# Half swaps of a rotating attention: keys ahead of the key spread, queries behind it

## The reference

```python
def _rope(x, base=ROPE_BASE):
    half = D // 2
    inv_freq = 1.0 / base ** (jnp.arange(half, dtype=jnp.float32) / half)
    ang = jnp.arange(S, dtype=jnp.float32)[:, None] * inv_freq[None, :]
    cos, sin = (jnp.cos(ang), jnp.sin(ang))
    x1, x2 = (x[..., :half], x[..., half:])
    return jnp.concatenate([x1 * cos - x2 * sin, x1 * sin + x2 * cos], axis=-1)
...
q = hidden_state @ Wq.T + bq
k = hidden_state @ Wk.T + bk
v = hidden_state @ Wv.T + bv
q = _rope(q)
k = _rope(k)
out = _banded_attention(split(q), split(k), split(v), WINDOW)
return out @ Wo.T + bo
```

## Time and profile before

| | us |
|---|---|
| median of 3 runs | 3945.59 (3945.36 to 3948.0) |
| profiled execution | 3952.28 |
| its span, first to last instruction | 3950.5 |
| first scores of L2a (T = 0) | at 2381.61 |
| scores of T = 30 | at 2633.14 |
| mean granted TensorE clock over the span | 0.929 of full speed |

### The profile page before, as it was taken

The page is one execution under the profiler, slowest core; times in us unless marked ns, Lnnn a source line. Parts: engine busy times, 40 slices in busy tenths (PEclk is TensorE's granted clock), DMA queues, the critical chain, the costliest instruction groups (busy, mean ns, idle before and its releaser), DMA issues. The chain is left out here.

```text
span 3950.5 us, 127503 instructions
## 1 busy us (share of the span) xinstructions
PE 3432.6 (87%) x46648; PEld 2618.2 (66%) x46648; DVE 2964.8 (75%) x6186; ACT 2252.1 (57%) x3856; POOL 1900.4 (48%) x3002
## 2 busy tenths in 40 slices
PE   8996886798899998999986938999989688789985
PEld 6885675465777775888875626888854344457764
DVE  6996995255898886888873476888867588659975
ACT  5775771344444444778862446778844466457653
POOL 6887984655441110224544425762223355357754
PEclk9997995899999998999986968999989799989988
DMA  2012213697000000110004821121112000000001
GB/s 83 29 31 79 66 58 93 187 266 205 20 17 3 1 0 23 52 52 21 17 21 137 255 80 46 48 55 53 52 46 61 15 0 0 0 28 26 26 8 43
DMA packets 321126, 227.48 MB, mean 58 GB/s; under 512 B 53712, under 2 KB 299472, under 8 KB 320720
## 3 DMA queue, kind: packets, MB, share of 16 engines
q1 hardware_dynamic: 261040, 174.96, 15.5%
q0 software_dynamic: 12288, 25.19, 2.1%
q10 hardware_dynamic: 47520, 23.60, 2.0%
HBM read 131.27 MB, written 54.53 MB: 47 GB/s over the span
## 5 line engine op out<-in xcount | busy, mean ns | idle before, releaser
L807 DVE TENSOR_REDUCE L2a_mx<-L2a_psS 128x32 f32<-128x2048 f32 x64 | 146.6, 2291 | 78.1 <-PE L2a_psS L593 78.1
L2501 POOL TENSOR_TENSOR L1a_rs<-L1a_ag,eps 128x1 f32<-128x1 f32 x64 | 13.0, 203 | 397.7 <-DVE L1a_ag L2666 397.7
L807 DVE TENSOR_REDUCE L1x_mx<-L1x_psS 128x32 f32<-128x2048 f32 x64 | 146.6, 2291 | 69.4 <-PE L1x_psS L593 69.4
L1138 POOL DMA_INDIRECT L0f_sorted_x<-X,L0f_IDX x128 | 123.0, 961 | 93.5 <-issue 34.1
L1557 DVE TENSOR_TENSOR L0f_G<-L0f_SG,L0f_psH 128x512 f32<-128x512 f32 x106 | 73.0, 689 | 112.6 <-ACT L0f_SG L1301 70.5
L493 POOL TENSOR_TENSOR L1x_rs<-L1x_mv,eps 128x2 f32<-128x2 f32 x64 | 12.5, 195 | 293.9 <-DVE L1x_mv L862 293.9
L782 ACT ACTIVATE L1x_PR<-L1x_PR 128x2048 f32<-128x2048 f32 x64 | 122.4, 1912 | 53.1 <-DVE L1x_PR L810 53.1
L810 DVE TENSOR_TENSOR L2a_PR<-L2a_psS,L2a_mx 128x2048 f32<-128x2048 f32 x64 | 146.7, 2292 | 7.3
L810 DVE TENSOR_TENSOR L1x_PR<-L1x_psS,L1x_mx 128x2048 f32<-128x2048 f32 x64 | 146.7, 2292 | 7.3
L782 ACT ACTIVATE L2a_PR<-L2a_PR 128x2048 f32<-128x2048 f32 x64 | 122.3, 1912 | 47.1 <-DVE L2a_PR L810 47.1
L719 ACT ACTIVATE L1x_PT<-L1x_psP 128x512 f32<-128x512 f32 x256 | 145.9, 595 | 2.8 <-PE L1x_psP L641 1.1
(11 more groups left out here) (620 smaller groups left out, 11506.1 us busy)
## 6 DMA issues: line engine op xcount, KB each, us to landing
L0f_WB<-in_w12a SPq DMA_DIRECT2D x53, 312.0 KB, 3.8
L0f_XB<-L0f_sorted_x SPq DMA_DIRECT2D x53, 256.0 KB, 4.0
L0f_sorted_y<-L0f_YB ACTq DMA_DIRECT2D x53, 256.0 KB, 3.9
L1m_WB<-in_w12b SPq DMA_DIRECT2D x37, 321.0 KB, 4.0
L1m_XB<-L1m_sorted_x SPq DMA_DIRECT2D x37, 256.0 KB, 4.1
L1m_sorted_y<-L1m_YB ACTq DMA_DIRECT2D x37, 256.0 KB, 4.2
L0x_VS<-in_ctx SPq DMA_DIRECT2D x64, 128.0 KB, 2.8
KB<-L1x_QK SPq DMA_DIRECT2D x256, 32.0 KB, 1.8
```

The source lines that it names most:

```text
L807: nc.vector.tensor_reduce(mx[:, T.u, :], sc, AX, ALU.max).then_inc(S["maxed"].sem, 1)
L1138: nc.gpsimd.indirect_dma_start(out=sorted_x[p][:, :], out_offset=bass.IndirectOffsetOnAxis(ap=IDX[:, k, t:t + 1], axis=0), in_=X[:, t, :], ...
L2501: nc.gpsimd.tensor_tensor(rs[:, A.par, 0:1], ag[:, A.par, 1:2], eps[:, 0:1], ALU.add).then_inc(S["var_eps"].sem, 1)
```

## The change

SyncE's swap becomes a small function that swaps one part, keys (0) or queries (1). In slot T the keys of pair T+2 are swapped first, after a wait for `o_k` of that pair, then comes the spread of pair T+1, then the queries of pair T+2 are swapped, after `o_q`. There are four swap transfers a slot where there were two, each of half the size (64 partitions by 256 values). The key swap counts on a semaphore that this attention did not use (`side_in`), the query swap on the old one (`stored`), and GpSimd's first rotation product waits for the former. The `pace` step (an increment of a semaphore) between SyncE's two waits for the swap is dropped. Other attentions are built without `halves` and keep their order.

```diff
@@ -346,6 +346,12 @@
 
 
             def sync(sp):
+                def swap_halves(M, part, copied, arrival):
+                    made(sp, copied, M.p + 1)
+                    for n in range(2):
+                        here, there = slice(64 * n, 64 * n + 64), slice(64 - 64 * n, 128 - 64 * n)
+                        sp.dma_start(RK[here, M.u, part, 256:512], RK[there, M.u, part, 0:256]).then_inc(parity_sem(arrival, M), 16)
+
                 def slot(T):
                     more = T.c + 4
                     if arrive and T.i is None and 0 <= more < MORE:
@@ -376,6 +382,8 @@
                         made(sp, "f_v", K.p - 1)
                         pace(sp, S)
                         sp.dma_start(CV[:, K.u, :], io["ctxT"][:, bass.ds(K.p * 256, 256)]).then_inc(parity_sem("side_in", K), 16)
+                    if halves and K.ok:
+                        swap_halves(K, 0, "o_k", "side_in")
                     B = T + ahead if turned else K
                     if B.ok:
 
@@ -385,13 +393,7 @@
                         for b in range(HQ):
                             sp.dma_start(KB[b:P:HQ, B.u, b, :, :].rearrange("p s k -> p (s k)"), KT[b:P:HQ, B.u, :]).then_inc(parity_sem("keys_in", B), 16)
                     if halves and K.ok:
-
-                        made(sp, "o_k", K.p + 1)
-                        pace(sp, S)
-                        made(sp, "o_q", K.p + 1)
-                        for n in range(2):
-                            here, there = slice(64 * n, 64 * n + 64), slice(64 - 64 * n, 128 - 64 * n)
-                            sp.dma_start(RK[here, K.u, :, 256:512], RK[there, K.u, :, 0:256]).then_inc(parity_sem("stored", K), 16)
+                        swap_halves(K, 1, "o_q", "stored")
                     if mask is by_key and K.ok:
                         made(sp, "side_made", 1)
                         pace(sp, S)
@@ -460,7 +462,7 @@
 
                         if not products_on_dve:
                             if halves:
-                                parity_wait(g, "stored", M, 32)
+                                parity_wait(g, "side_in", M, 32)
                             else:
                                 made(g, "o_k", M.p + 1)
                             rope_product(nc.gpsimd, M, 0, ck).then_inc(S["gates"].sem, 1)
@@ -887,7 +889,7 @@
             count(dict.fromkeys(("f_tx", "f_q", "f_v", "o_tx", "o_q"), PAIRS), not by_rows)
             count(dict(rope_parts=4 * PAIRS, rope_sums=2 * PAIRS, ctx_normed=PAIRS, rows_in0=8 * PAIRS, rows_in1=8 * PAIRS, ctx_in0=16 * PAIRS, ctx_in1=16 * PAIRS), by_rows)
             count(dict.fromkeys(("q_roped", "k_roped", "gates_out", "gates"), PAIRS), turned)
-            count(dict(stored0=16 * PAIRS, stored1=16 * PAIRS), halves)
+            count(dict(stored0=16 * PAIRS, stored1=16 * PAIRS, side_in0=16 * PAIRS, side_in1=16 * PAIRS), halves)
             count(dict(side_made=1, w_in0=32 * PAIRS, w_in1=32 * PAIRS), mask is by_key)
             count(dict(xres=PAIRS), bias_row is not None)
             count(dict(mix=PAIRS), not rows_on_dve)
```

## The result

The changed kernel takes 3985.97 us (median of 6 runs, 3983.68 to 3989.64) against 3946.13 us (6 runs) for the kernel before: +39.8 us, a ratio of 1.0102 with a 95% interval of 1.0088 to 1.0117. It is slower, as forecast, by 39.8 where 33.7 were forecast. The forecast time was 3979, the range 3964 to 3996. In the profiled executions the span went from 3950.5 to 3987.8 us.

A forecast was written before the change was run, and what follows sets the result against it. Bounds were the swap-spread ring, 8.13 us a slot, beside TensorE's 7.94; a new 9.30 us ring would decide. Stage 286.2 against 251.5, less 0.95 at the start, is +33.7 us: 3979 us, range 3964 to 3996.

The forecast's parts named there:

- The ring: Layer 2's rotating attention: scores, key projection, copy, key swap issue, spread, next scores close a loop of 9.30 us a slot.
- five legs: Scores to copy end 3.75, copy to swap issue 0.03, two issues 1.33, gap to spread 0.25, spread to scores 3.94 us.
- TensorE's 7.94: TensorE's own work in one slot: 8.17 us less 0.23 idle, a bound beside the loop of waits before the change.
- the old ring: Kernel before: key spread, swap, GpSimd's rotation and key sum, next spread; 8.13 us a slot, opened by the change.
- the case from which the upper end of the range was built: The spread, with key-swap traffic just ahead, lands as slowly as a swap: 0.33 us a slot, 10 us.
- The stalls and the start: Spreads issued or landing late count in full, 6.8 us; the stage's first spread comes earlier, gaining 0.95 us.
- TensorE's 14 idles for the spread: First score matmul, 2485 to 2615 us before the change: 1.5 + 1.2 = 2.7 us idle, named cause the key spread.
- The query swap: Issued behind the spread on SyncE, needed by GpSimd only in the next slot: nothing waits, cost 0.
- The rival that it works as meant: SyncE's key swap fits ahead of the spread without delaying it, both old waits go: some 3942 us; chance 8 in 100.
- The prediction's ring of 7.97 without the issues: The new loop on SyncE with the two swap issues counted near nothing: 9.30 - 1.33 = 7.97 us a slot.
- The clock: Rival: TensorE idling 1.36 us a slot drops its clock in every second slot, 21 us more, 4000 us; 8 in 100.
- a sum of 286.2: Scores(0) to scores(30): 204.6 loop, 53.6 unrolled, 21.2 first two slots, 6.8 late spreads, against 251.5 us now.

The follow-up runs named there:

- the wait alone: The kernel before, with SyncE waiting for the key copy of pair T+2 ahead of the spread of T+1 and no swap moved: 3955.01 us, 1.0009.
- the filled run: The changed kernel with eight extra 128x128 transposes a slot on TensorE behind the value projection: 3976.93 us, 1.0073 times the kernel before.

## Why the prediction was right

*The ring.* Right. Its five legs were forecast as 3.75, 0.03, 1.33, 0.25 and 3.94 us, and stand at 3.71, 0.03, 1.10, 0.25 and 3.86 in the slot shown. The one term that was mis-sized is the pair of issues: a swap of half the size is issued in a median of 0.56 us, 1.10 for two, where I carried over the 1.33 of the full swap. That is 9.05 for 9.30 us a slot. That it is the issues, and neither the wait nor the landing, is shown by four runs: without them (the wait alone) the slot is 8.08, with 0.46, 1.10 and 2.45 us of them 8.41, 9.05 and 10.40. From 0.46 us on, each us of issue ahead of the spread is a us of the slot; without any, that line would give 7.95, and the 8.08 lies between TensorE's 7.94 and the old ring's 8.13, so there another bound decides. Nor does the spread land later for the key swap just ahead of it, the case from which the upper end of the range was built: 3.86 us to the scores against 3.94.

*The stalls and the start.* The first scores start at 2380.92, 0.69 earlier, while the stage itself starts 0.47 later (first key copy at 2370.54, not 2370.07): a gain of 1.16, forecast 0.95. That all late spreads would count in full was not tested by itself. The long slots left in the filled run fit it, but don't show it. One reading of the prediction is loose and carries nothing: of TensorE's 14 idles for the spread, puts 8, with 1.5 of the 2.7 us, down to issue and not to the spread.

*The query swap.* Right: GpSimd waits for neither swap.

*The rival that it works as meant* failed where the prediction said, at the 0.52 us into which the issue had to fit. The rule that a DMA's start is small beside the DMA itself, which the Trainium skill gives (DMA: Bandwidth & Descriptors, Issuing engines are not separate DMA queues), doesn't help on this path: 1.10 us of issue for the pair stands beside 2.0 us from an issue to its landing (the median in the changed kernel), and all of it was paid. The other half of the same sentence held: issuing from another engine saves the sequencer's time, and that was worth the whole loss (3937.9 us against 3985.97). The prediction's ring of 7.97 without the issues would still have stood 0.03 us above TensorE's 7.94, which changes nothing in the case.

*The clock.* Here the prediction was wrong. It gave 8 in 100 to a falling clock, as a case by itself, on the strength of a stretch in which TensorE is 85% busy at a clock of 1.00. It fell in part: T = 2 to 8 and three later slots began or ran at the lower level. T = 2 to 8 take 75.9 us (2402.35 to 2478.26), where the prediction's ring and 5.0 of its 6.8 us of late spreads gave 4 x 8.93 + 3 x 9.30 + 5.0 = 68.6; in the filled run, at the upper clock, they take 67.8. Over the whole, from T = 0 to 30, it is 291.6 us against a sum of 286.2: the lower clock in T = 2 to 8 and in the slots from 2532.58 and 2597.24 added nearly 10 us that the sum didn't have, and the shorter issues (17 slots by 0.25) took off some 4. So that 39.8 lies as near to 33.7 as it does is in part luck, two errors of opposite sign. The step that failed is the inference from an equal busy share: from 420 to 590 us, with TensorE busy 144.00 of 170 us, the clock was 1.00, and of the two later windows shown above, with 25.71 and 26.80 of 30 us busy, it was 1.00 in the first and 0.94 in the second. What about the idles here lets the clock fall in the slot from 2532.58, and not in its neighbours with the same idle of 1.0 to 1.2 us, stays open.

## What to carry to other kernels

Before a transfer is moved ahead of another in the same queue, add up the issue time of what is moved and compare it with the gap between the moment its wait ends and the moment the other would have been issued; 1.10 us did not fit into 0.52, and the difference came back in every slot because the scores close the ring. If the early start is wanted, issue it from a queue whose engine waits anyway, or put it behind. And when a change leaves TensorE idle once in each slot, price the lower clock as part of the forecast, not as a remote rival.

## What the runs showed of the hardware

An issue of a transfer of 64 rows of 1 KB takes SyncE 0.46 to 0.60 us (median 0.56) in the changed kernel, and in the run where ScalarE issues it ScalarE's queue 0.47 to 0.85 (median 0.50). With twice the rows, in the kernel before, it takes SyncE 0.64 (median), and with half of them, four transfers in 2.45 us, 0.59. So the price goes nearly by the number of issues and not by their rows. Eight transposes a slot that nobody reads, in an idle of 1.0 to 1.2 us, held the granted clock at 1.00 and made the changed kernel faster, 1.0073 instead of 1.0102 times the kernel before: the extra work gave back some 11 us.
